# A layer kernel with two routed expert layers: stores of split weights on ScalarE's queue, one expert more split inside the expert loop, a residual added on TensorE, and two type conversions left out of the routing chain

## The reference

```python
x = x + 0.5 * ffn(layernorm(x), ...)
x = x + attention(layernorm(x), ...)
x = x + 0.5 * ffn(layernorm(x), ...)

def ffn(x, norm_w, gate_w, gate_b, w1, b1, w2, b2):      # 16 experts, top 4
    t = x * rsqrt(mean(x * x) + EPS) * norm_w
    logits = t @ gate_w.T + gate_b
    vals, idx = top_k(logits, 4)
    G = zeros.at[idx].set(softmax(vals))
    h = einsum("mh,eoh->emo", t, w1) + b1                # 256 -> 512
    a, b = min(h[..., ::2], 7), clip(h[..., 1::2], -7, 7)
    act = a * sigmoid(1.702 * a) * (b + 1)
    y = einsum("emi,edi->emd", act, w2) + b2             # 256 -> 256
    return x + einsum("me,emd->md", G, y)
```

## Time and profile before

| | us |
|---|---|
| median of 3 runs | 881.34 |
| range of the 3 runs | 877.83 to 882.27 |
| the profiled execution's own time | 881.05 |
| its span, first to last instruction | 879.3 |

### The profile page before, as it was taken

One profiled execution on the slowest core, in us unless ns is written; L12 is line 12 of the kernel. 1 busy time (PEld: TensorE's weight loads), 2 busy tenths in 40 slices (PEclk: granted clock), 3 DMA queues, 4 the chain that ended last, 5 costly groups with the idle time before them and its releaser, 6 DMA issues.

```text
span 879.3 us, 17231 instructions
## 1 busy us (share of the span) xinstructions
PE 684.1 (78%) x4630; PEld 542.7 (62%) x4630; DVE 617.2 (70%) x1482; ACT 429.1 (49%) x916; POOL 466.0 (53%) x451
## 2 busy tenths in 40 slices
PE   1534518899999999157899898897279999999990
PEld 1322316688888887055676676665158888888870
DVE  5756917777777776335777877775867777777777
ACT  3534404555555555114676666654335555555550
POOL 4836762666656667441234534444625666666671
PEclk9999999999999999657999999977569999999995
DMA  8967985568888861544444323316645778876755
GB/s 306 357 257 294 371 290 179 192 221 281 272 301 289 290 220 54 170 147 144 144 145 165 137 104 130 116 48 240 207 138 198 258 253 274 269 249 224 246 209 210
DMA packets 87417, 189.11 MB, mean 215 GB/s; under 512 B 13008, under 2 KB 37856, under 8 KB 85792
## 3 DMA queue, kind: packets, MB, share of 16 engines
q1 hardware_dynamic: 47440, 119.57, 39.1%
q0 software_dynamic: 13872, 40.01, 12.3%
q10 hardware_dynamic: 26016, 28.42, 10.8%
HBM read 105.46 MB, written 65.72 MB: 195 GB/s over the span
## 4 chain that ended last, share of the span: by engine, by line
PE 36%; DVE 14%; issue 3%; POOL 2%; ACT 1%; DMA 0%; DVEq 0%; ACTq 0%
PE s_psT L888 12%; PE s_psG L910 6%; DVE s_a_nm L1616 4%; PE s_psG L1336 3%; PE s_psS L1364 2%; PE s_psS L855 2%; PE s_psS L869 2%; PE s_psO L1399 2%; POOL rows L1279 2%; DVE all_x L2067 2%; PE s_psG L1349 1%; PE s_psT L1380 1%; PE s_psR L1503 1%; PE s_psT L1384 1%; DVE s_a_xp L1584 1%
## 5 line engine op out<-in xcount | busy, mean ns | idle before, releaser
L1051 POOL DMA_INDIRECT kbuf<-f_e_ys,f_e_place x80 | 83.3, 1042 | 71.8 <-ACT f_e_ys L1001 64.8
L888 PE MATMUL f_bank<-f_e_w,f_e_th 128*128 x320 | 118.0, 466 | 2.0 <-ACT f_e_th L1024 0.9
L1051 POOL DMA_INDIRECT kbuf<-s_e_own_ys,s_e_own_place x80 | 82.3, 1028 | 67.6 <-ACT s_e_own_ys L1001 60.4
L888 PE MATMUL s_psT<-s_e_own_w,s_e_own_th 128*128 x320 | 115.4, 460 | 0.9 <-ACT s_e_own_th L1024 0.9
L1279 POOL DMA_INDIRECT rows<-s_a_row,s_a_slot_i x64 | 63.3, 989 | 89.2 <-DVE s_a_slot_i L1744 72.5
L1616 DVE TENSOR_REDUCE s_a_nm<-s_psS 128x4 f32<-128x1024 f32 x64 | 78.3, 1224 | 45.4 <-PE s_psS L1364 45.3
L941 DVE TENSOR_TENSOR s_e_own_hb<-s_psT,s_e_own_bias 128x512 f32<-128x512 f32 x80 | 55.3, 691 | 43.3 <-PE s_psT L888 43.1
L587 POOL DMA_INDIRECT rows<-f_r_row,f_r_slot_i x64 | 65.1, 1017 | 37.0 <-DVE f_r_slot_i L525 18.5
L941 DVE TENSOR_TENSOR f_e_hb<-f_bank,f_e_bias 128x512 f32<-128x512 f32 x80 | 55.1, 689 | 35.3 <-PE f_bank L888 35.3
L1883 ACT ACTIVATE s_a_pT<-s_psT 128x1024 f32<-128x1024 f32 x62 | 63.4, 1023 | 27.7 <-PE s_psT L1384 27.4
L888 PEld LDWEIGHTS f_bank<-f_e_w,f_e_th 128*128 128x128 f32 x320 | 61.5, 192 | 23.6 <-issue 5.5
(11 more groups left out here) (337 smaller groups left out, 1808.3 us busy)
## 6 DMA issues: line engine op xcount, KB each, us to landing
w_split<-stage SPq DMA_DIRECT2D x11, 1536.0 KB
f_e_w<-w_split SPq DMA_DIRECT2D x24, 512.0 KB, 4.6
s_e_own_w<-w_split SPq DMA_DIRECT2D x24, 512.0 KB, 4.3
f_e_tb<-rows ACTq DMA_DIRECT2D x80, 144.0 KB, 3.4
s_e_tb<-rows ACTq DMA_DIRECT2D x80, 144.0 KB, 3.1
stage<-w_raw SPq DMA_DIRECT2D x11, 768.0 KB, 10.8
s_a_part<-kbuf SPq DMA_DIRECT2D x8, 1024.0 KB, 5.4
s_a_qs<-s_a_qk SPq DMA_DIRECT2D x32, 256.0 KB, 2.6
```

The lines of the kernel that those rows point to most:

```text
L888: last = pe.matmul(psH[j][:, :], left[:, p % 2, j, k * P:(k + 1) * P], w1[:, bass.ds(buf, 1), h, k * I2:(k + 1) * I2], start=n == 0, stop= ...
L1051: pool.indirect_dma_start(out=kbuf[:, :], out_offset=bass.IndirectOffsetOnAxis(ap=place[:, n:n + 1], axis=0), in_=ys[:, n, :], in_offset=N ...
```

## The change

Five things are changed.

1. **Stores.** `split.store` of experts 4 to 10 leaves SyncE's list. ScalarE issues them: in group g it issues, after its exponential, the stores of the staged experts of turn g - 1. SyncE keeps the loads.
2. **Which expert where.** `FIRST` and `SHARE` now give the turns [4,5], [6,0], [7,1], [8], [9,2], [10], [3], []. Expert 11 is split inside the loop; `IN_LOOP` has 15 parts in place of 12, at the same places up to step 4, three at step 5 and three at step 6 where there were one and two. ScalarE loads expert 14 and stores 12 at step 3, loads 15 at step 4, stores 11 at step 1; SyncE stores 13 and 14 later in the loop. SyncE loads 11, 12 and 13 after its paddings.
3. **Residual.** TensorE adds x itself: after each product with b2 it multiplies x by the identity into the same PSUM tile (`start=False`). ScalarE copies the tile to x (`kept`), for group g - 1 inside group g and for the last group before its paddings. VectorE's `add_biases` is gone in the first layer.
4. **Conversions.** `topf` and `slot_k` are no longer written: the comparison reads the unsigned indices `topi`, and the reduction writes the integers `slot_i`. This is done in both expert layers.
5. **Offsets.** The running `token` is replaced by a table `places`, made once on GpSimd. Also in both layers.

```diff
-        pool.iota(c["place0"][:, :], pattern=[[1, GPT]], base=-T, ...
+        pool.iota(c["places"][:, :, :], pattern=[[GPT * P, NG], [1, GPT]], base=-T, ...
-    FIRST = (4, 5, 6, 0, 7, 8, 1, 9, 10, 2, 11, 3, 12, 13, 14, 15)
+    FIRST = (4, 5, 6, 0, 7, 1, 8, 9, 2, 10, 3, 11, 12, 13, 14, 15)
-    SHARE = (2, 2, 2, 1, 2, 1, 1, 1)
+    SHARE = (2, 2, 2, 1, 2, 1, 1, 0)
...
         for e in (4, 5, 6, 0, 1, 2, 3):
             split.load(sp, e)
-        split.store(sp, 4)
-        split.store(sp, 5)
         split.load(sp, 7)
         sp.wait_ge(s_bias, 16)
         first_biases(sp)
-        for e in range(6, 12):
-            split.store(sp, e)
-            split.load(sp, e + 2)
-        split.load(sp, 14)
+        for e in (8, 9, 10):
+            split.load(sp, e)
         sp.wait_ge(s_ends, 1)
         pad_rows(sp, m.phase, table, rows, c, s_pad, FIRST, some=range(NE // 2))
+        for e in (11, 12, 13):
+            split.load(sp, e)
...
-            ch.link(dve.tensor_copy(topf[:, :, :], topi[:, :, 0:TOP]))
             ch.link(dve.tensor_tensor(hot[:, :, :, :], c["ramp_e"][:, None, None, :].to_broadcast(full),
-                                      topf[:, :, :, None].to_broadcast(full), ALU.is_equal))
+                                      topi[:, :, 0:TOP, None].to_broadcast(full), ALU.is_equal))
...
-            ch.done(dve.tensor_scalar(token[:, :], token[:, :], float(GPT * P), None, ALU.add))
...
-            ch.link(dve.tensor_reduce(slot_k[:, :, :], mix[:, :, :, :], X_AXIS, ALU.add))
             dve.wait_ge(s_gates, g + 1)
-            dve.tensor_copy(slot_i[i][:, :, :], slot_k[:, :, :]).then_inc(s_slot, 1)
+            with nc.allow_low_precision("whole numbers"):
+                dve.tensor_reduce(slot_i[i][:, :, :], mix[:, :, :, :], X_AXIS, ALU.add).then_inc(s_slot, 1)
...
+        def kept(g):
+            xv = x[:, g * GPT:(g + 1) * GPT, :].rearrange("p t d -> p (t d)")
+            act.wait_ge(s_b, g + 1)
+            act.activation(xv, psB, ACT.Copy).then_inc(s_x, 1)
...
             act.activation(ex[:, :, :], diff[:, :, :], ACT.Exp).then_inc(s_ex, 1)
+            if g > 0:
+                for e in in_cycle[g - 1]:
+                    if e >= split.DIRECT:
+                        split.store(act, e)
+                kept(g - 1)
...
+        kept(NG - 1)
         act.wait_ge(s_ends, 1)
         pad_rows(act, m.phase, table, rows, c, s_pad, FIRST, some=range(NE // 2, NE))
...
-                last = pe.matmul(psB[:, t * D:(t + 1) * D], gT[:, t * P:(t + 1) * P], c["b2"][:, :], start=True, stop=True)
+                pe.matmul(psB[:, t * D:(t + 1) * D], gT[:, t * P:(t + 1) * P], c["b2"][:, :], start=True, stop=False)
+                if t == 0:
+                    pe.wait_ge(s_res, g + 1)
+                last = pe.matmul(psB[:, t * D:(t + 1) * D], c["ident"][:, :], x[:, g * GPT + t, :], start=False, stop=True)
...
-               (3, 0): [(14, 0)], (3, 1): [(14, 1)], (4, 0): [(14, 2)], (5, 0): [(15, 0)], (6, 0): [(15, 1)], (6, 1): [(15, 2)]}
-    STORES_SP, SECOND_LAG = {7: 13, 10: 14, 13: 15}, 2
+               (3, 0): [(13, 0)], (3, 1): [(13, 1)], (4, 0): [(13, 2)], (5, 0): [(14, 0)], (5, 1): [(14, 1), (14, 2)],
+               (6, 0): [(15, 0), (15, 1)], (6, 1): [(15, 2)]}
+    STORES_SP, SECOND_LAG = {9: 13, 11: 14, 13: 15}, 2
...
+            if first_layer and s == 3:
+                split.load(act, 14)
+                split.store(act, 12)
...
             if first_layer and s == 1:
-                split.store(act, 12)
-            if first_layer and s == 3:
+                split.store(act, 11)
+            if first_layer and s == 4:
                 split.load(act, 15)
```

More of the change, by code:

```diff
@@ L1714, in routed_order @@
             ch.after()
-            ch.link(dve.scalar_tensor_tensor(row[i][:, :, D + NE:ROWC], order[:, :, :], float(T), token[:, :, None].to_broadcast([P, GPT, NE]), ALU.mult, ALU.add))
-            ch.done(dve.tensor_scalar(token[:, :], token[:, :], float(GPT * P), None, ALU.add))
+            ch.link(dve.scalar_tensor_tensor(row[i][:, :, D + NE:ROWC], order[:, :, :], float(T), c["places"][:, g, :, None].to_broadcast([P, GPT, NE]), ALU.mult, ALU.add))
         def routed_weights(g):
```

33 lines of the change are left out of this document (10 added, 23 removed).

## The result

The changed kernel took 875.37 us (median of 20 runs, 870.54 to 880.7), the kernel before in the same comparison 878.96 (20 runs). The ratio is 0.9958, 95% interval 0.9941 to 0.9976: a gain of 3.6 us or 0.4%, where 9.7 was forecast. The profiled execution of the changed kernel has a span of 875.0 us (before 879.3). In two of the five sets in which the experiments ran, the kernel before took 918.8 and 920.75 us where it takes 878 to 880 in the others (the expectations call this slow chips), so every ratio is taken to the before of its own set.

A forecast was written before the change was run, and what follows sets the result against it. Routing was taken to be bound by GpSimd's sends, held up by late loads behind stores in SyncE's queue. Routing -8.4, loop +2.0 and attention -3.3 made -9.7 from 881.05, so 871.3 us; range 863.5 to 877.5.

The forecast's parts named there:

- Rival 1: Routing: only the bytes count, one store and one load fewer save 5.2 us; 874.6 us in all, chance 0.13.
- Rival 4: Conversions return inside two instructions (874.6 us), or step 4 waits for store 12 and paddings are late (874 to 876); 0.16.
- the second term of the sum: Expert loop: added parts cost 1.2 us in step 5 and 0.8 in step 6, +2.0 us.
- Routing: -8.4 forecast: Routing: both paths, GpSimd's sends and ScalarE's list, end at 116.5 to 116.9 where the fetch was at 125.10.
- Steps (a) to (d): Routing: first store 30.4, load 7 at 37.4, group 2's exponential 48.3, GpSimd's wait 6 to 7 us, last send 112.6.
- Step (e)'s second path: Routing's end on ScalarE: group 7's exponential at 90.5, products 4.1 us a group, 8 paddings 8.3 us, end at 116.5.
- Step (b): Routing: with turn 2 as [7, 1], the exponential of group 2 at 48.3 in place of 53.66, 5.3 us earlier.
- Steps 0 to 4 keep their pattern: Expert loop: the bigger table of parts adds nothing to steps 0 to 4.
- The bound named for store 12: Loop step 4: load 15 may wait for store 12 to land, up to 3 us; taken as 0.
- Attention: -3.3 forecast: Attention and second routing: 0.46 us less a group for groups 0 to 5, 2.8, and 0.5 for group 6.
- Rival 2: Routing: the first stall goes too through faster landings, last send at 106, 15 us earlier; 863.7 us, chance 0.15.
- Rival 3: Routing: three queues starve the sends; at 28 us of landing 18 us are lost, 889 us; chance 0.06.

The follow-up runs named there:

- issue_late: The changed kernel with load 14 and store 12 of loop step 3 issued behind that step's high part; 874.6 us, ratio 0.993.
- stores_act_3: The kernel before with routing's stores on ScalarE's queue and the new order of experts; 871.68 us, ratio 0.9921.
- twelve: The changed kernel with expert 11 split in routing again and the loop's table, stores and loads of before; 869.21 us both times, ratios 0.987 and 0.9885.
- all three edits together: The changed kernel with load 14 and store 12 behind step 3's high part, one part a place, load 15 at step 5; 871.68 us, ratio 0.9923.

## Why the prediction was right and wrong

The range (863.5 to 877.5) held the 875.4, and the direction was right. That the range held it is luck in so far as its upper end was set for rivals 1 and 4 and the scatter, and not for the loss that came. The size was not, and the step that failed is the second term of the sum.

**Routing: -8.4 forecast; -7.8 at the first fetch, -8.5 at the first loop step.** Steps (a) to (d) were 2 to 4 us too late each: ScalarE's queue ran ahead of its arithmetic, so the first store went at 27.96 and not at 30.4, load 7 at 33.6 and not at 37.4, the exponential of group 2 at 45.3 and not at 48.3, and GpSimd waited 4.1 us and not 6 to 7. The last send was 1.8 us earlier than forecast (110.8 for 112.6). One error made that good: the landing behind the last send was taken over at 4.3 us, and it was 6.5. So that the fetch came out 0.4 us from the forecast is in part luck. Step (e)'s second path was no limit: 8 paddings took 4.2 us and not 8.3, and the last entry was issued by 108.7 and not at 115. One of its terms was too small: the products with b2 and with x took 4.9 us a group (19.5 and 19.6 us over eight groups) and not 4.1. Step (b), that expert 8 leaves turn 2, is what the first stall hung on; the loads did not come earlier.

**Loop: +2.0 forecast, +8.4 and +6.9 measured in two profiles, of which +7.0 and +7.4 in steps 0 to 9.** This is the step that failed. Steps 5 and 6 were to take 7.4 and 7.6; they took 8.56 and 7.53, 1.1 us more than forecast in sum. Steps 3 and 4, put at nothing, took 3.8 us more than in before. "Steps 0 to 4 keep their pattern" was the mistake: the table of parts kept it, but the issues of load 14 and store 12 had moved ahead of a high part in step 3, and I costed only the wait for a landing at step 4, none for the issues and none for what a stop of VectorE costs TensorE. The bound named for store 12 (it may take 10 us to land, then up to 3 us) was the right mechanism, seen at 9.9 us between store 12 and load 15 and 5.3 us of waiting in issue_late. In after the loss was in front of it.

**Attention: -3.3 forecast, -3.7 as the mean of the profiles.** The mechanism is right: a batch is shorter by 0.5 us where 0.46 was forecast. The mean of the whole stage has too much chance in it to say more than that it agrees.

**The rivals.** Rival 1, that only the bytes count, would have given 874.6 us, near what was measured, and is still wrong: stores_act_3 moves the bytes of before and has its first fetch 6.0 us earlier. The Trainium skill, "DMA: Bandwidth & Descriptors", section "Issuing engines are not separate DMA queues", says that DMAs from several engines run on the same 16 DMA engines; the trace agrees in that the peak stayed at 445 GB/s for 455. The 6.6 us of stores_act_3 (871.68 for 878.3) are no measurement against that section, since they hold the order of the experts as well as the queue. The rows show both at work: the order ahead of group 2, the queue at load 9. Rival 2 is half true: the first stall did not go but fell to a third. It gave faster landings as the reason, and loads 7 and 8 were no faster; its sum also takes +1 for the loop where the forecast has +2, with no reason given. Rival 3 did not come: the median landing of a send went from 6.2 us to 5.9. Rival 4 named waits at step 4; its conversions half is refuted, its half on waits is of the right kind at the wrong step.

**What I had not looked at** is whether taking expert 11 out of routing gains anything. Behind the table VectorE and ScalarE wait for the sends to land, so its splitting was hidden there but for 1.2 to 1.8 us at the first step; in the loop nothing hides it. Without the loop's term my sum would have been -11.7; twelve measured -10.6 and -9.8.

## What to carry to other kernels

Work is cheapest where its engine waits for something else that is far longer: the expert that was put ahead of VectorE's wait of some 23 us cost 6 us more in the loop. When a stream of loads and stores shares one in-order queue, look for the entry that waits and for what is queued behind it, and then for what stands behind the wait: here the longest stall went because the wait for load 8 was moved behind the exponential, though the load itself came 2 us later. And when a move looks free because its table row is unchanged, count each DMA that it issues ahead of work for another engine. Removing one such wait only uncovered the next, and all three edits together gave back half of the 7.0 us that the first ten steps had lost.
